# Turned attention scores in two matmul products instead of four, with the inputs placed by DMA and the engines' orders rewritten

## What is computed

```python
# layer 0
q = split_heads(x @ Wq.T); k = split_heads(text @ Wk.T); v = split_heads(text @ Wv.T)
x = merge(softmax(q @ k.T / 4) @ v) @ Wo.T + bo + x
# layer 1: 73 text tokens, 4 image tokens
probs = softmax(q @ k_text.T / 4); text_out = probs @ v_text
sem = l2norm(probs @ text) @ l2norm(ip).T
probs_ip = softmax(q @ k_ip.T / 4 + 0.5 * sem) * mask
x = merge(text_out + probs_ip @ v_ip) @ W_out + b_out + x
```

## Time and profile before

| | us |
|---|---|
| median of 3 runs | 2448.57 |
| lowest, highest | 2446.62, 2458.31 |
| the profiled execution | its own time is not listed; its span from first to last instruction is 2447.7 |
| PE, PE weight loads | 2259.4, 1464.0 busy |
| DVE, ACT, POOL | 1702.0, 1728.4, 1592.2 busy |
| DMA | 310.92 MB, mean 127 GB/s |

### The profile page before, as it was taken

One profiled execution on the slowest core, in us unless ns is written; L12 is line 12 of the kernel. 1 busy time (PEld: TensorE's weight loads), 2 busy tenths in 40 slices (PEclk: granted clock), 3 DMA queues, 4 the chain that ended last, 5 costly groups with the idle time before them and its releaser, 6 DMA issues.

```text
span 2447.7 us, 90636 instructions
## 1 busy us (share of the span) xinstructions
PE 2259.4 (92%) x35896; PEld 1464.0 (60%) x35896; DVE 1702.0 (70%) x2860; ACT 1728.4 (71%) x2604; POOL 1592.2 (65%) x1056
## 2 busy tenths in 40 slices
PE   8999958999999999999999999999999999999984
PEld 6777735655566665666556555666566655555642
DVE  5543425777777777777777777777777777777763
ACT  4332327778878777787787787877877787787861
POOL 4121135777777777777777776777777777777762
PEclk9999969999999999999999999999999999999996
DMA  9968622444444444444344444444444444444421
GB/s 275 281 209 235 194 89 70 117 115 117 118 114 114 118 115 116 118 115 117 111 118 119 115 114 114 113 118 115 115 118 118 114 113 115 114 119 116 119 80 56
DMA packets 338318, 310.92 MB, mean 127 GB/s; under 512 B 180224, under 2 KB 281856, under 8 KB 337920
## 3 DMA queue, kind: packets, MB, share of 16 engines
q1 hardware_dynamic: 337920, 305.36, 44.7%
HBM read 164.66 MB, written 105.98 MB: 111 GB/s over the span
## 4 chain that ended last, share of the span: by engine, by line
PE 46%; DVE 23%; ACT 7%; issue 5%; DMA 3%; SPq 2%; DVEq 0%; POOL 0%; ACTq 0%; POOLq 0%
PE psum L1065 12%; PE psum L966 10%; PE psum L1049 8%; PE psum L1028 7%; DVE q_low L1220 4%; ACT q_high L1136 4%; DVE mneg L1213 3%; PE psum L969 3%; ACT ef L1154 3%; DVE e L1235 3%; DVE sq L1254 2%; DVE outt L1313 2%; PE psum L1032 2%; PE psum L991 2%; DVE x1b L1313 1%
## 5 line engine op out<-in xcount | busy, mean ns | idle before, releaser
L1381 POOL TENSOR_TENSOR e<-ef,eh 73x1024 f32<-73x1024 f32 x320 | 681.1, 2129 | 300.4 <-ACT eh L1169 257.0
L1154 ACT ACTIVATE ef<-psum 73x1024 f32<-73x1024 f32 (+1 forms) x640 | 628.0, 1011 | 90.9 <-PE psum L1032 87.4
L1235 DVE TENSOR_TENSOR e<-psum,e 73x1024 f32<-73x1024 f32 x320 | 386.7, 1209 | 135.6 <-PE psum L1065 135.3
L1213 DVE TENSOR_REDUCE mneg<-psum 128x8 f16<-128x616 f32 (+3 forms) x512 | 446.9, 923 | 34.9 <-PE psum L991 34.1
L1065 PE MATMUL psum<-eh,gram 128*73 128x512 f16 x1280 | 340.9, 390 | 45.2 <-ACT ef L1154 16.0
L1049 PE MATMUL psum<-ef,values 128*32 128x256 f32 x5120 | 351.4, 389 | 7.7 <-DVE pip L1295 5.9
L1028 PE MATMUL psum<-q_high,keys 32*73 32x256 f16 (+2 forms) x6144 | 324.7, 258 | 34.0 <-DVE mneg L1213 21.6
L1169 ACT ACTIVATE eh<-ef 73x1024 f16<-73x1024 f32 x320 | 337.0, 1053 | 16.2 <-ACT ef L1154 0.4
L1220 DVE SCALAR_TENSOR_TENSOR q_low<-psum,q_high 128x640 f16<-128x640 f32 x128 | 105.5, 824 | 262.3 <-ACT q_high L1136 262.3
L1028 PEld LDWEIGHTS psum<-q_high,keys 32*73 32x73 f16 (+1 forms) x6144 | 186.9, 110 | 144.5 <-issue 68.7
L1162 ACT ACTIVATE ust<-psum 128x512 f32<-128x512 f32 x384 | 223.4, 594 | 67.1 <-PE psum L1049 60.5
(11 more groups left out here) (180 smaller groups left out, 4530.3 us busy)
## 6 DMA issues: line engine op xcount, KB each, us to landing
rb<-r_dram SPq DMA_DIRECT2D x128, 384.0 KB, 4.1
keys<-k_dram SPq DMA_DIRECT2D x128, 231.0 KB, 3.6
values<-v_dram SPq DMA_DIRECT2D x128, 192.5 KB
ust<-ust SPq DMA_DIRECT2D x512, 48.0 KB, 2.5
v_dram<-vst SPq DMA_DIRECT2D x64, 320.0 KB
out<-outt SPq DMA_DIRECT2D x64, 320.0 KB, 2.2
k_dram<-kst SPq DMA_DIRECT2D x32, 616.0 KB, 4.8
x<-in_x SPq DMA_DIRECT2D x32, 384.0 KB, 3.7
```

The source lines that it names most:

```text
L1154: act.activation(ef[l][0:m, unit_heads(n), :].rearrange("t h s -> t (h s)"), src, ACT.Exp, scale=SM).then_inc(s_exp[l], 1)
L1213: dve.tensor_reduce(dst, o, AX_X, ALU.max, negate=True).then_inc(s_max[l], 1)
L1235: dve.tensor_tensor(rest, banks(l, f"u{k}", 2)[0:m, :, :], rest, ALU.mult).then_inc(s_wr, 1)
L1381: pool.tensor_tensor(e2[0:m, k, :, :], ef[1][0:m, unit_heads(k), :], eh[0:m, unit_heads(k), :], ALU.subtract).then_inc(s_e2, 1)
```

## The change

The turned scores become two groups of matmuls instead of four. Heads are now interleaved in each 32-partition group: even partitions one head, odd the other. For one parity the left operand of the first product (`ka`) has a head's key parts in the rows of both parities (high in one, low in the other) and the right operand `tq` has the head's high queries in both, so one product gives high x high and low x high. The second product multiplies the high keys and rows of marks (`ks`) by the low queries and the negated maxima. For this `turn_queries` spreads the two query parts by two moves of 128 x 2560 bytes per layer, and `place_maxima` puts the maxima over the rows of the other parity by two moves of 96 KB. Keys are loaded by three moves (`load_key_tiles`). Keys are stored in the first stage without zeros, once, in 8 batches per move.

The numerators go in one move of 64 partitions. The inverses are still stored in two copies, and spread by two moves of 64 partitions into one `rb` that both layers share. The small columns for the semantics are loaded with the gram rows. Residuals are made in place in a ring of six inputs, from which the output is stored too. Part of a query, output or gram product may start when only its first bank is free (`only=0`). All five orders and the banks are new; waits for banks are now taken from PE's unrolled order.

```diff
     "pe": """
-        1u2/3 1a1/3 0t1/1 1q/2 0t2/1 0a0/1 1s0/2 0a1/1 1s1/2 0a2/1 1a2/3 1i/2 1u3/3 1m/2 1u4/3 1t0/2 0q/0
-        1n0/3 1n1/3 1p/4 0s0/0 1n2/3 1n3/3 1n4/3 0s1/0 1t1/2 1a0/2 1u0/2 1t2/2 1u1/2 1o/4 0m/0 0o/1 0t0/0""",
+        0t2/1 0a0/1 0a1/1 1s0/2 0a2/1 1u3/3 1s1/2 0q/0 1m/2 1i/2 1a2/3 1p/4 1u4/3 1n0/3 1n1/3 0s0/0 1n2/3 1n3/3 1n4/3
+        1t0/2 0s1/0 1o/4 1y/3 1t1/2 1u0/2 0m/0 0o/1 1t2/2 1a0/2 1u1/2 0t0/0 1a1/2 1u2/2 0t1/0 1q/1""",
...
     "sp": """
-        1ss/3 1sl/3 1rl/4 1sh/4 0x/0 1vi/4 1ps/4 0ds/1 1v/2 1pl/4 1ds/3 0k/0 0rw/1 0sh/1 0rl/1 1g/2 1c/1
-        0v/0 1ns/3 1rw/3 1nl/3 1k/1 1d/3 1st/4""",
+        0x/0 1sh/4 0k/0 1ps/4 1tq/2 0ds/1 1pl/4 0sh/1 0rw/1 1tm/2 0rl/1 1ds/3 0tq/0 1v/2 1ns/3 1d/3 1nl/3 1st/4 1rw/3
+        0tm/0 1sl/3 0v/0 1k/1 1ss/2 1vi/1 1g/1 1rl/3""",
...
+def load_key_tiles(sp, ka, ks, src, loaded):
+
+    both_parts = src.rearrange("a x (r f) n -> (a r) x (f n)", f=2)
+    sp.dma_start(ka[:].rearrange("p f n -> p (f n)"), both_parts).then_inc(loaded, 16)
+    for e in (0, 1):
+        high = src[:, 0, 1 - e:P:2, :].rearrange("a r n -> (a r) n")
+        sp.dma_start(ks[1 - e:P:2, e, :, :], high.unsqueeze(1).to_broadcast([HALF, 2, KC])).then_inc(loaded, 16)
...
+                dst = [k_dram[l][bass.DynSlice(batch, CB), :, :, :].rearrange("b x p n -> x p b n") for l in both]
+                for l in both:
+                    results_of("k", l, 1)
+                    for x in (0, 1):
+                        keys = kst[l][:, x, :, :, :].rearrange("p b c t -> p b (c t)")
+                        sp.dma_start(dst[l][x, :, :, 0:2 * T], keys).then_inc(s_kstored, 16)
+                results_of("kt", 0, 1)
+                for l in both:
+                    for x in (0, 1):
                         for copy in (0, 1):
-                            tail = ktail[l * HALF:(l + 1) * HALF, half, :, :, :, :].rearrange("p b h e t -> p b (h e t)")
-                            sp.dma_start(dst[l][copy * HALF:(copy + 1) * HALF, :, 8 * T:], tail)\
-                              .then_inc(s_kstored[half], 16)
+                            sp.dma_start(dst[l][x, copy * HALF:(copy + 1) * HALF, :, 2 * T:],
+                                         ktail[l * HALF:(l + 1) * HALF, x, :, :]).then_inc(s_kstored, 16)
...
+            def turn_queries(l, b, n):
+
+                b.reached(sp, f_t[l], CW, 0)
+                b.reached(sp, s_ql[l], 1, 1)
+                for e in (0, 1):
+                    rows = qq[l][1 - e:P:2, :, :].rearrange("p h n -> p (h n)")
+                    sp.dma_start(tq[l][:, e, 0:2 * QW], rows.unsqueeze(1).to_broadcast([HALF, 2, 2 * QW]))\
+                      .then_inc(s_tq[l], 16)
+
+            def place_maxima(l, b, n):
+
+                b.reached(sp, s_tq[l], 32, 32)
+                b.reached(sp, s_mt[l], 1, 1)
+                for e in (0, 1):
+                    dst = tq[l][e:P:2, e, QW:].rearrange("p (c s) -> p c s", c=CW)
+                    sp.dma_start(dst, mt[l][e:P:2, :].unsqueeze(1).to_broadcast([HALF, CW, S])).then_inc(s_tm[l], 16)
...
-                for j in range(NJ):
-                    sp.dma_start(ust[l][j * SLOT + D:(j + 1) * SLOT, b.parity(), 0, :, :],
-                                 ust[l][j * SLOT:j * SLOT + D, b.parity(), 1, :, :]).then_inc(s_num[l], 16)
+                sp.dma_start(ust[l][1:P:2, b.parity(), 0, :, :], ust[l][0:P:2, b.parity(), 1, :, :]).then_inc(s_num[l], 16)
...
+                for copy in range(COPIES):
+                    dst = r_dram[l][b.parity()][:, copy, :].rearrange("j (q i) -> j q i", i=QS)
                     sp.dma_start(dst, rd[l][:, b.parity(), :]).then_inc(s_rw[l], 16)
 
             def spread_inverses(l, b, n):
                 b.reached(sp, s_at[l], 1, 0)
-                b.reached(sp, s_rw[l], 32, 32)
-                src = r_dram[l][b.parity()].rearrange("h k n -> (h k) n").unsqueeze(1).to_broadcast([2 * HC, D // 2, CW * S])
-                sp.dma_start(rb[l][:].rearrange("p c s -> p (c s)"), src).then_inc(s_rb[l], 16)
+                before = spread_before(l, b)
+                if before is not None:
+                    sp.wait_ge(s_at[before[0]], before[1] + 1)
+                b.reached(sp, s_rw[l], 16 * COPIES, 16 * COPIES)
+                for r in (0, 1):
+                    src = r_dram[l][b.parity()][:, :, r * CW * S:(r + 1) * CW * S].rearrange("j c n -> (j c) n")
+                    src = src.unsqueeze(1).to_broadcast([NJ * COPIES, D // COPIES, CW * S])
+                    sp.dma_start(rb[r:P:2, :, :].rearrange("p c s -> p (c s)"), src).then_inc(s_rb[l], 16)
...
-                    for low, q in ((0, qh[l]), (0, ql[l]), (1, qh[l])):
-                        for rows, o in tiles:
-                            pe.matmul(o, keys(l, low, c)[rows, e, 0:n], q[rows, cols], start=(low == 0 and q is qh[l]),
-                                      stop=False)
+                        cols = slice(2 * S, PW)
                     for rows, o in tiles:
-                        k, lead = (2 * c + e, 0) if c < 2 else (2 * c, e * many)
-                        mm = pe.matmul(o, sel[rows, k, 0:n], mt[l][rows, lead:lead + many], start=False, stop=True)
+                        pe.matmul(o, paired_keys(l, e, c)[rows, 0:n], tq[l][rows, e, cols], start=True, stop=False)
+                    for rows, o in tiles:
+                        mm = pe.matmul(o, marked_keys(l, e, c)[rows, 0:n], tq[l][rows, e, QW:2 * QW][:, cols], start=False,
+                                       stop=True)
...
+                    ins = act.activation(data[:, c, :], data[:, c, :], ACT.Identity, bias=bias_sb[l][:, c:c + 1])
```

More of the change, by code:

```diff
@@ L35 @@
 HD = 24
[L36 removed]
+GC = TXT[1]
+GW = GC + IP
+COPIES = 2
+DEN = 1
+KC = CW * T
+QW = PW
+TW = QW + CW * S
+RING = 6
 QT = 4
@@ L166, with step_of, in_order @@
-LAGS = max(lag for engine in ORDER for _, lag, _, _ in steps_of(engine))
[8 rows of a table added]
+]
+def step_of(word):
+    step, number = word.split("/")
+    name = step[1:].rstrip("0123456789")
+    return int(step[0]), int(number), name, int(step[1 + len(name):] or 0)
+def in_order(engine):
+    cycle = [step_of(word) for word in ORDER[engine].split()]
+    begin = [step_of(word) for word in FIRST.get(engine, "").split()]
+    end = [(l, B - 1 - before, name, n) for l, before, name, n in map(step_of, LAST.get(engine, "").split())]
+    lags = max(lag for _, lag, _, _ in cycle)
+    middle = [(l, i - lag, name, n) for i in range(B + lags) for l, lag, name, n in cycle if 0 <= i - lag < B]
+    whole = begin + middle[len(begin):len(middle) - len(end)] + end
+    assert sorted(whole) == sorted(middle)
+    return whole
@@ new lines, in __init__, with filled @@
+        last = [None] * BANKS
+        for l, batch, name, n in in_order("pe"):
+            for use in self.filled(l, name, n):
+                for r in self.banks(l, use[1:]):
+                    self.earlier[use, batch, r], last[r] = last[r], (use, batch)
+    @staticmethod
+    def filled(l, name, n):
+        if name in ("s", "t"):
+            return [f"{l}{name}{k}" for k in (2 * n, 2 * n + 1) if name == "s" or k < UNITS]
+        if name == "n" and n:
+            return []
+        return [f"{l}{name}{n}" if name in ("a", "u") else f"{l}{name}"]
@@ L190, in wait, with banks @@
+    def banks(self, l, use):
+        return [r for r in range(BANKS) if f"{l}{use}" in self.on[r]]
+    def wait(self, eng, sems, b, l, *uses, only=None):
         wanted = {}
-        for use in (f"{l}{u}" for u in uses):
-            for line in self.on:
-                if use not in line:
+        for use in uses:
+            mine = self.banks(l, use)
+            for r in mine if only is None else mine[only:only + 1]:
+                if self.earlier[f"{l}{use}", b.index(), r] is None:
                     continue
-                k, back = line.index(use), 0
-                while True:
-                    k, back = (k - 1, back) if k else (len(line) - 1, back + 1)
-                    last = line[k]
-                    earlier = b.later(self.lag[use] - back - self.lag[last])
-                    if not b.fixed or 0 <= earlier.i + earlier.off < B or b.i + b.off + self.lag[use] - back < 0:
-                        break
-                if b.fixed and not 0 <= earlier.i + earlier.off < B:
-                    continue
+                last, batch = self.earlier[f"{l}{use}", b.index(), r]
@@ L204, in wait @@
                 kind = last[1:].rstrip("0123456789")
                 name, each, k = self.READ[kind]
-                k = k or int(last[1 + len(kind):]) + 1
+                count = each * batch + (k or int(last[1 + len(kind):]) + 1)
                 key = int(last[0]), name
-                if key not in wanted or wanted[key][0].off * each + wanted[key][2] < earlier.off * each + k:
-                    wanted[key] = (earlier, each, k)
-        for (layer, name), (earlier, each, k) in wanted.items():
-            earlier.reached(eng, sems[name][layer], each, k)
```

(5 more changed lines are left out.)

362 lines of the change are left out of this document (168 added, 194 removed), and 16 rows, old and new, of the table USES.

## The result

The changed kernel takes 2604.05 us (median of 4 runs, 2596.98 to 2613.89), the kernel before beside it 2447.6 (2445.38 to 2458.31): 1.063 times as long, 95% interval 1.060 to 1.067. The forecast was 2362 us, faster.

What follows compares the result with a forecast made beforehand. It took the per-batch chain round the engines, not nearly full PE, as the bound: 13.7 + 16.6 = 30.3 us, 1.27 less, times 67.7 is 86 off 2447.7, giving 2362 us. Own range 2310 to 2410; 80% range 2290 to 2450.

Steps and rivals of the forecast that it cites:

- Under 30.3 that is cover: SP's issuing per batch rises from 20.6 to 24 us, hidden under the 30.3 us period, so costs nothing.
- rival "no change": Rival 4: SP serves in order; 24 us of issuing with waits may take today's 31.5 us: 2448 us; chance 0.08.
- The chain from sums to output product: Attention stage, sums through denominators, inverses and spread to high half: 13.7 us instead of 15.1 per batch.
- ACT's way back: ACT's 20 instructions from high half to the next third piece of sums: 16.6 us per batch.
- The round trips to PE: Within ACT's way back, layer 0's first turned scores and layer 1's query: about 0.8 us put back.
- Handover of the sums to SP: From ACT's sums to SP's issue of the denominators: 0.1 us.
- PE's saving: Fewer turned-score matmuls save 2.2 us per batch, at most 149 us; counted at nothing because the chain is longer.
- The waits for maxima on PE: Turned scores waiting for the moved maxima: 0 to 1 us per period, taken as nothing.
- a small piece is about a quarter of a large one: First stage's key stores: four times the pieces cost about the same, so zero change.
- Rival 2: Small pieces bind the first stage: some 40 us over eight slots, 2402 us; chance 0.10.
- The rule of the Trainium skill: Key stores below 512 B fall to read-modify-write, off line rate; by it 2402 us, kept at 0.10.
- Rival 3: Query moves delay denominators and spread: period 32.9 us, 2538 us; sign: denominators landing after 3 us; chance 0.14.

Runs made afterwards that it cites:

- The old kernel with the issues alone: Kernel before plus the eight new query and maxima moves per batch, read from a constant tile without new waits: 2630.16 us, period 34.38 us.
- the queue free: Changed kernel with keys loaded and query parts and maxima moved for the first batch only: 2456.36 us, period 31.29 us.

## Why the prediction was wrong

*The step that failed for most of it: "Under 30.3 that is cover".* SP's issuing was costed by its total against the period. It is a queue served in order, and an issue is free only where nothing urgent stands behind it. The old kernel with the issues alone loses 2.8 us per batch; in the changed one the fourteen issues of keys and turning, with their waits, are worth 2.19 of the 3.2 us by which 33.48 exceeds 30.3. The other 1.0 is there with the queue free, 0.8 of it in ACT's way back. The total was also short: 27.6 us, not 24, since the new issues take 0.6 to 1.0 each. The rival "no change" named this mechanism, and priced it as if it could only eat the gain.

*The chain from sums to output product* was right: 13.6 us against the same 13.6 (13.7 with the handover of 0.1), denominators to inversion 2.6 against 2.9, stores' end to spread 1.6 against 2.1, spread to POOL's start 4.7 against 3.9; the 3.1 us of numerator issues between are gone.

*ACT's way back* was 16.6 in the forecast, 17.5 with a free queue (handover included), 18.0 in the changed kernel. The round trips to PE cost more than the 0.8 allowed: four waits add up to 2.1 us in the period read. One of them, 1.02 us, was for turned scores which had waited 1.12 for DVE's weighted gram, itself behind the norms' return from HBM (4.2 and 2.3 us to land): a path the sum never walked. Weighting the gram first was to remove this wait and came out slower, so how much of the difference is this path stays open.

*Handover of the sums to SP* was 0.1 in the forecast and 1.5 in the trace. Together: 13.7 + 16.6 = 30.3 has become 13.6 + 18.0 + 1.5 = 33.1.

*PE's saving* was put at nothing beside the chain, and that held in the old kernel: 12 us. In the new order it is worth 1.1 us per batch, so the loss would be larger without it. PE's busy time per batch fell to 0.856 x 33.48 = 28.6 us, not to 27.8. The waits for maxima on PE, taken as zero, were small (3.7 us, in one wait). The waits that took their place were SP's, 48.7 us for the turned maxima `mt` and 123.3 for turned scores.

*The input load* was not in the walk at all. Its ring let it go earlier, its place in the order did not. In the one profile it is 0.25 us per batch, within noise.

*First stage: "a small piece is about a quarter of a large one".* The row said that 512 small pieces land as fast as 128 large ones; that is the latency of one move on idle engines. On full engines each piece takes its 50 ns. Rival 2 had the mechanism, and a price above the measured one: 40 us against 24.7 in the profiled run, from 7 to 28 in the others. The rule of the Trainium skill, "DMA: Bandwidth & Descriptors", Specifications, stood with it, and I let one landing time outweigh it.

*Rival 3, slower by the bulk moves' bytes,* had the sign and not the cause. DVE inverted the denominators 2.6 us after their issue, against 2.3 before, short of the 3 us named as its sign; DMA's share rose to 0.53, not 0.65; and the bytes are worth 0.67 of the 1.91 us. The outcome lay outside the range because no rival added a slower first stage to a slower loop.

## What to carry to other kernels

Cost every DMA issue that is added to a queue by what stands behind it there, walking the queue once round with start times, and not by the queue's busy share. Before trading matmuls for moves, leave the matmuls out of the old kernel and time it: here that gives 12 us, 0.18 us of each period, where one of the fourteen issues taken away is worth 2.19 / 14 = 0.16 in the mean. Count packets, not bytes, where a stage's transfers come near full share, and read a packet's time from a stretch where the engines are full.

## What was not expected of the hardware

- A packet of the hardware queue takes 50 ns of a DMA engine at 920 bytes mean and at 417, and 70 ns at 1404. This is an occupancy as the profile books it: between 50 and 150 us of the changed kernel the packets' times add up to 117% of the 16 engines, so some overlap.
- An issue lengthens when the engines are behind: 0.40 us in the median (up to 2.06) for the old key stores, 2.31 (up to 4.80) for the new ones.
- An issue on ACT's queue is not free to ACT: a pair of the maxima's moves takes 1.3 to 1.5 us there, once 2.2, and ACT starts nothing meanwhile.
- A round trip through HBM costs 6.5 us for 128 KB out and a part of it back: 4.2 to land the norms, 2.3 to fetch them.
